# Who splits the shared weight tiles into bf16 pairs, and when the first expert rows are loaded

## The reference

```python
x = x + xattn(layernorm(x), ctx)      # per batch: q, k = ctx @ Wq.T + bq, ctx @ Wk.T + bk
                                      # attention = softmax(q @ k.T); x_m = layernorm(x) @ attention.T
h = layernorm(x)
probs = softmax(h @ gate_w.T)         # 8 experts, the best 2 are kept and renormalised
moe = sum_e combine[e] * (silu(h @ w_gate[e]) * (h @ w_up[e])) @ w_down[e]        # 352 units each
shared = (silu(h @ sw_gate) * (h @ sw_up)) @ sw_down                              # 1408 units
x = x + moe + shared * sigmoid(h @ shared_gate_w)
```

## Time and profile before

| | |
|---|---|
| median of 3 runs | 754.27 us (753.54 to 779.26) |
| the profiled execution | 755.93 us |
| its span in the profile | 754.1 us |
| mean granted clock of TensorE | 0.968 of full speed |
| PE busy | 706.1 us (94%) |
| DVE busy | 344.2 us (46%) |
| ACT busy | 233.7 us (31%) |
| POOL busy | 187.8 us (25%) |
| DMA | 70.99 MB, mean 94 GB/s |

### The profile page before, as it was taken

How to read it: one execution, slowest core, us unless ns; L and a number is a source line. 1 busy time by engine, 2 the same in 40 slices (tenths; PEclk the granted TensorE clock), 3 DMA queues, 4 the chain that set the end, 5 groups by cost and what they waited for, 6 DMA issues and landing times.

```text
span 754.1 us, 10855 instructions
## 1 busy us (share of the span) xinstructions
PE 706.1 (94%) x3808; PEld 381.1 (51%) x3808; DVE 344.2 (46%) x753; ACT 233.7 (31%) x387; POOL 187.8 (25%) x147
## 2 busy tenths in 40 slices
PE   7949979799999999999999899799999999999991
PEld 5525434244454454454444344366666666666660
DVE  3998566514352536452558754363333333333320
ACT  2515013011531132531344343233333333333320
POOL 2372057801400002200244600012222222222221
PEclk8978999899999999999999999899999999999997
DMA  8422022612300003200146972435455445444532
GB/s 281 139 83 84 1 83 85 249 56 84 115 1 0 1 1 112 87 1 1 40 149 226 319 242 76 135 95 90 85 86 86 87 85 86 85 84 87 87 43 28
DMA packets 45749, 70.99 MB, mean 94 GB/s; under 512 B 3577, under 2 KB 25337, under 8 KB 45698
## 3 DMA queue, kind: packets, MB, share of 16 engines
q1 hardware_dynamic: 33570, 41.42, 18.6%
q0 software_dynamic: 10544, 27.30, 16.6%
q10 hardware_dynamic: 1584, 1.57, 0.7%
HBM read 42.99 MB, written 27.29 MB: 93 GB/s over the span
## 4 chain that ended last, share of the span: by engine, by line
PE 83%; DVE 10%; DMA 2%; issue 2%; ACT 1%; SPq 1%; POOL 0%; ACTq 0%; DVEq 0%; POOLq 0%
PE bank L1449 26%; PE bank L1508 19%; PE bank L1464 13%; PE bank L1532 10%; PE bank L1297 4%; PE bank L1496 2%; PE bank L1245 2%; DVE arena L831 2%; PE bank L1519 2%; PE bank L1254 1%; DVE hx_odd L831 1%; PE bank L1267 1%; DVE arena L1135 1%; DMA silu_sb<-L_ffn_shared_gate_w 1%; PE bank L1311 1%
## 5 line engine op out<-in xcount | busy, mean ns | idle before, releaser
L1449 PE MATMUL bank<-hT,arena 128*128 128x512 f16 x1056 | 244.3, 384 | 8.4 <-DVE prod L1152 8.4
L1449 PEld LDWEIGHTS bank<-hT,arena 128*128 128x128 bf16 x1056 | 103.6, 99 | 133.4 <-DVE prod L1152 10.0
L1508 PE MATMUL bank<-arena,ctx_sb 128*128 x936 | 152.2, 312 | 0.0
L1464 PE MATMUL bank<-arena,hidden 128*128 128x512 bf16 x528 | 123.5, 386 | 0.0
L1508 PEld LDWEIGHTS bank<-arena,ctx_sb 128*128 128x128 f16 x936 | 91.2, 97 | 50.0 <-issue 0.2
L570 POOL DMA_INDIRECT out<-staging,token_blk x39 | 60.6, 1553 | 188.3 <-ACT staging L785 184.4
L1197 DVE TENSOR_TENSOR hidden<-bank,hidden 128x384 bf16<-128x384 f32 x39 | 21.7, 557 | 153.9 <-ACT hidden L777 153.9
L1464 PEld LDWEIGHTS bank<-arena,hidden 128*128 128x128 bf16 x528 | 52.1, 99 | 63.4 <-issue 6.7
L1532 PE MATMUL bank<-arena,hidden 128*128 (+1 forms) x351 | 82.2, 379 | 1.5 <-DVE hidden L1197 1.5
L785 ACT ACTIVATE staging<-bank,w_blk 128x512 f32<-128x512 f32 x39 | 26.8, 687 | 122.7 <-PE bank L1532 122.7
L1152 DVE TENSOR_TENSOR prod<-silu_sb,bank 128x512 f32<-128x512 f32 x44 | 30.1, 685 | 73.7 <-PE bank L1449 73.6
(11 more groups left out here) (181 smaller groups left out, 690.4 us busy)
## 6 DMA issues: line engine op xcount, KB each, us to landing
hx_odd<-xs_dram SPq DMA_DIRECT2D x39, 262.0 KB, 2.8
staging<-L_ffn_w_gate SPq DMA_DIRECT2D x6, 704.0 KB, 4.9
staging<-L_ffn_w_up SPq DMA_DIRECT2D x6, 704.0 KB, 5.1
arena<-x SPq DMA_DIRECT2D x3, 1024.0 KB, 7.4
out<-arena POOLq DMA_DIRECT2D x3, 1024.0 KB, 4.7
staging<-L_ffn_w_down SPq DMA_DIRECT2D x6, 512.0 KB, 4.0
staging<-L_ffn_sw_gate SPq DMA_DIRECT2D x11, 256.0 KB, 3.0
staging<-L_ffn_sw_up SPq DMA_DIRECT2D x11, 256.0 KB, 3.5
```

The source lines that it names most:

```text
L1449: op = nc.tensor.matmul(ps[:, :], weights[:, j, wp, kind, c * P:(c + 1) * P], hT[:, t % 2, hp, c, :], start=(c == 0 and s == 0), stop=(c = ...
L1464: op = nc.tensor.matmul(out_ps[i][:, :], hidden[:, j % 3, hp, i * P:(i + 1) * P], weights[:, j, wp, DOWN, :], start=(j == 0 and s == 0), s ...
L1508: op = nc.tensor.matmul(ps[:, 0:I], xT[:, k % 2, xp, c * P:(c + 1) * P], arena[:, bass.ds(at + (part_at(0, part) + wp * low_gap(part) + c ...
```

## The change

It has three parts.

1. POOL splits only tiles 0 to 3 (`POOL_TILES`). Its first split waits for `attn_ready` (batch 0's attention rows scaled), its third for `normed_ready[0]` of batch 1, its fourth for `normed_ready[1]` of batch 0. `routing_constants` stands first.
2. Tiles 4 to 10 are split in block 0 by ACT (`unit_tile_high`) and DVE (`unit_tile_low`) at the points of `TILES_AT`. Each side counts on semaphores of its own, and `wait_split` picks the right one for PE and SP. `assign` moves from (1, "gate") to (1, "down").
3. SP loads the rows of blocks 0 to 2 after 19 pieces of weights instead of after 24.

```diff
@@ AT_POINT_FIRST
-    (1, "gate"): [("assign", 0), ("attn_low", 0)],
+    (1, "gate"): [("attn_low", 0)],
     (1, "up"): [("attn", 0), ("attn", 1), ("attn", 2), ("attn", 3)],
+    (1, "down"): [("assign", 0)],
...
+POOL_TILES = 4
+TILES_AT = {
+    (2, "up"): [4], (3, "up"): [5], (4, "gate"): [6], (5, "up"): [7], (6, "up"): [8], (7, "up"): [9],
+    (8, "up"): [10],
+}
+LOAD_BLOCKS_BEFORE = 19
...
+        def wait_split(eng, j):
+            if j < POOL_TILES:
+                eng.wait_ge(split_pool, j + 1)
+            else:
+                eng.wait_ge(split_dve, j + 1 - POOL_TILES)
...
                 if j >= 2:
-                    sp.wait_ge(split, j - 1)
+                    wait_split(sp, j - 2)
...
+            for q in range(LOAD_BLOCKS_BEFORE):
                 load_piece(q)
-
             sp.wait_ge(table_ready, 1)
...
+            for k in range(3):
+                load_block(k)
+            for q in range(LOAD_BLOCKS_BEFORE, PIECES):
+                load_piece(q)
+            for k in range(3, NBLK):
+                load_block(k)
...
+            routing_constants()
             inverse_deviation(0, 0)
+            pool.wait_ge(attn_ready, RT)
             split_unit_tile(0)
+            split_unit_tile(1)
             inverse_deviation(0, 1)
-            split_unit_tile(1)
-            routing_constants()
+            pool.wait_ge(normed_ready[0], RT * 2)
+            split_unit_tile(2)
             inverse_deviation(1, 0)
-            for j in range(2, 5):
+            pool.wait_ge(normed_ready[1], RT)
+            for j in range(3, POOL_TILES):
                 split_unit_tile(j)
             inverse_deviation(1, 1)
-            for j in range(5, UT):
-                split_unit_tile(j)
             fill_spare()
...
+            def unit_tile_high(j):
+
+                act.wait_ge(staged[j % 2], 16 * 3 * (j // 2 + 1))
+                if j == BORROWED:
+                    act.wait_ge(hlo_ready, KC * 2)
+                nc.scalar.copy(weights[:, j, HI, :, :], staging[:, j % 2, :, :]).then_inc(high_split_act, 1)
...
+                    if t == 0:
+                        for n in TILES_AT.get((j, point), ()):
+                            unit_tile_high(n)
...
+            def unit_tile_low(j):
+
+                dve.wait_ge(high_split_act, j + 1 - POOL_TILES)
+                nc.vector.tensor_tensor(weights[:, j, LO, :, :], staging[:, j % 2, :, :], weights[:, j, HI, :, :],
+                                        ALU.subtract).then_inc(split_dve, 1)
```

More of the change, by code:

```diff
@@ L371, in build_xattn_moe @@
         r_step, exp_in_ready, r_exp = sem("r_step"), sem("exp_in_ready"), sem("r_exp")
-        high_split, split = sem("high_split"), sem("split")
+        high_split_pool, split_pool = sem("high_split_pool"), sem("split_pool")
+        high_split_act, split_dve = sem("high_split_act"), sem("split_dve")
         gate_done, up_done, down_done = sem("gate_done"), sem("up_done"), sem("down_done")
@@ L428, in load_piece @@
                 elif slot < 2:
-                    sp.wait_ge(split, UT)
+                    wait_split(sp, UT - 1)
                 else:
@@ L461, in _, with load_block @@
                 load_unit_tile(j)
-            for q in range(PIECES):
+            def load_block(k):
+                if k >= 3:
+                    sp.wait_ge(xt_turned, k - 2)
+                    sp.wait_ge(meta_ready, k - 2)
+                at = sp.value_load(table[0:1, 0, k:k + 1], min_val=0, max_val=DUMP - P)
+                sp.dma_start(xblk[:, k % 3, :], xs_dram[bass.ds(at, P), :]).then_inc(x_in[k % 3], 16)
+            for q in range(LOAD_BLOCKS_BEFORE):
                 load_piece(q)
@@ L469, in _ @@
             sp.wait_ge(pads_sent, 16 * E)
-            for k in range(NBLK):
-                if k >= 3:
-                    sp.wait_ge(xt_turned, k - 2)
-                    sp.wait_ge(meta_ready, k - 2)
-                at = sp.value_load(table[0:1, 0, k:k + 1], min_val=0, max_val=DUMP - P)
-                sp.dma_start(xblk[:, k % 3, :], xs_dram[bass.ds(at, P), :]).then_inc(x_in[k % 3], 16)
+            for k in range(3):
[4 more added lines that the diff above has]
+                load_block(k)
         @block.gpsimd
@@ L512, in fill_spare @@
                                    pad_row[:, :]).then_inc(spare_filled, 16)
-            arrived = [0, 0]
             def split_unit_tile(j):
                 slot = j % 2
-                arrived[slot] += 16 * 3
-                pool.wait_ge(staged[slot], arrived[slot])
-                if j == BORROWED:
-                    pool.wait_ge(hlo_ready, KC * 2)
-                nc.gpsimd.tensor_copy(weights[:, j, HI, :, :], staging[:, slot, :, :]).then_inc(high_split, 1)
-                pool.wait_ge(high_split, j + 1)
+                pool.wait_ge(staged[slot], 16 * 3 * (j // 2 + 1))
+                nc.gpsimd.tensor_copy(weights[:, j, HI, :, :], staging[:, slot, :, :]).then_inc(high_split_pool, 1)
+                pool.wait_ge(high_split_pool, j + 1)
                 nc.gpsimd.tensor_tensor(weights[:, j, LO, :, :], staging[:, slot, :, :], weights[:, j, HI, :, :],
-                                        ALU.subtract).then_inc(split, 1)
+                                        ALU.subtract).then_inc(split_pool, 1)
             def inverse_deviation(which, b):
@@ L1141, in beside @@
                     attention(t, j, point)
+                    if t == 0:
+                        for n in TILES_AT.get((j, point), ()):
+                            unit_tile_low(n)
                     for q in PIECES_AT.get((t, j, point), ()):
@@ L1474, in ffn_block @@
                 for j in range(UT):
-                    pe.wait_ge(split, j + 1)
+                    wait_split(pe, j)
                     pe.wait_ge(silu_ready, t * UT + PRIME + j)
```

## The result

The changed kernel takes 723.07 us, median of 4 runs (722.17 to 726.31), against 754.9 (753.54 to 779.26) for the kernel before: 0.9593 of its time, 95% interval 0.9559 to 0.9627. The ratio leaves out the run of 779.26, an execution in a slower state of the chip; the median of the other three runs of before is 754.27, and 31.2 us lie between the two kernels. The forecast was 723, range 717 to 732.

What follows compares the result with a forecast made beforehand. PE, busy 94%, was held by waits for DVE, whose SBUF-to-SBUF work waited for POOL's splits. Gains of 9.4 + 6.6 + 8.1 - 0.4 + 7.4 = 31.1 us off the median 754.27 gave 723, range 717 to 732.

Steps and rivals of the forecast that it cites:

- Rival (d): L831 is slow for another reason than POOL, so only the expert entry gains: 747 us; chance 0.03.
- Part 1: Front, to about 60 us: no split beside either slow L831 group, gain 9.4 us, bounds 8 and 11.5.
- Rival (b): Front doesn't gain: POOL's splits slide onto the normalisations or the clock stays low longer, 732 us; chance 0.08.
- Parts 2 and 3: Batch 1's normalisation, gain 6.6 us, and second router, gain 8.1 us: PE's waits there go.
- The cover of 2.2: Batch 1's normalisation: L831 ends 2.2 us before PE finishes its down product; lateness within that costs nothing.
- Part 4: Other moved work: splits on ACT and DVE cost 0, `assign` 0.4 us, the pad fill 0.
- the ring: Two staging slots for unit tiles: a slot's next tile is wanted 15.5 us later, takes 8.2, cover 7 us.
- (a): Tile 6 lands late behind pads and rows, and PE waits 11 us once: 734 us; chance 0.06.
- (c): Turns of the two staging slots take far longer than 8.2 us; at 36 the time is 774 us; chance 0.01.
- Part 5: Expert entry: rows issued ahead of weight piece 19 remove PE's 4.6 us wait; gain 7.4 us, low bound 5.
- what would show it: Signs of being right: L831 near 0.5 us each, no `prod` wait above 1.5, clock 1.00 from 60 on.

Runs made afterwards that it cites:

- e4: Changed kernel plus six GpSimd copies, SBUF to SBUF, beside batch 1's second normalisation: 727.21 us, one run.
- e9: Changed kernel plus six GpSimd memsets, which only write, beside batch 1's second normalisation: 729.73 us, one run.
- e11: Changed kernel with front and expert entry of the kernel before (POOL splits tiles 0 to 4 without waits, rows late): 742.77 us, 0.9833 of before.
- e5: Changed kernel run again unaltered, as yardstick on another chip: 723.55 us, 0.9586 of before.
- e3: Changed kernel without POOL's three waits that hold its splits back: 730.47 us, 0.9686 of before.
- e1: Kernel before with only the rows of blocks 0 to 2 issued after 19 weight pieces: 749.03 us, 0.9931 of before.
- e10: Changed kernel with `assign` back at (1, "gate"): 723.88 us, one run.
- e2: Changed kernel with the rows of blocks 0 to 2 again behind all 24 weight pieces: 730.28 us, 0.9676 of before.
- e6: Changed kernel with POOL splitting only tiles 0 to 2, tile 3 going to ACT and DVE: 722.78 us, 0.9576 of before.
- e8: e7 plus PE turning the shared gate's rows behind batch 0's two projections: 717.53 us, 0.9506 of before.
- e7: e6 plus the routing's `tables` part 2 moved from (2, "gate") to (2, "down") in later blocks: 719.98 us, 0.9535 of before.

## Why the prediction was right

**The bound.** That three of four long waits came from POOL's splits, not from the work of DVE itself, is shown: L831 is back at 1.9 wherever POOL is quiet, and at 6.4 where e4 or e9 makes it busy. That the third of these waits, at the second router, goes with the moved splits is shown by e11. Rival (d) is out.

**Part 1** was 1.1 too small, with the terms off both ways. The 11.2 came whole. L822 lost 1.3 instead of 1.7, because it came 0.96 later than before while the two pairs ended at 35.75, 0.65 later than I had put them; the second L822 lost 0.2 instead of 0.4, L854 0.2 instead of 0.3. That is 9.5; what is left of the 10.53, some 1.0, I put down to the clock, for which I had 0.6. It stayed at full level in this execution (1.00 from 44 to 52), and the first product took 2.75, where the timeline of before has 3.39 (3.19 in the earlier trace rows, by the count of the chain). In e5 it was 0.75 from 46 to 48 and 0.50 from 48 to 50, the product took 3.16 and the stretch 28.89: there the clock's term is 0.5. Rival (b) didn't come, but its mechanism is real: e3, with POOL's waits taken away, has the splits back on the normalisations, and is 7.4 slower, of which 5.9 lie in this stretch.

**Parts 2 and 3** hold within 0.1 as a sum: 14.37 for 14.3 (6.6 + 8.1, less the 0.4 of `assign`), in the changed kernel and again in e11. With the 0.2 that `assign` cost they gave 14.6 for 14.7. The cover of 2.2 was 2.0 (L860 ends at 88.6, PE turns the rows at 90.60). The second router's chain from logits to `prod` is 8.7 us (106.29 to 115.02) for a forecast of some 10, so its cover was 3.3 instead of 3.

**Part 4.** `assign` cost 0.2 for 0.4. The pad fill cost DVE nothing, as taken, though it ran beside L860 itself. No DVE subtraction and no ACT cast made PE wait: the ring never ran dry, and rivals (a) and (c) have nothing in the trace.

**Part 5** gave 7.78 for 7.4, in the changed kernel and in e1 alone. The 0.4 that I had put down as given back by the last splits isn't seen.

**What was wrong.** By the profiled execution the sum was 1.5 too large, 31.1 for 29.6. That the median came within 0.1 us of the forecast is in part luck: the four runs of the changed kernel spread over 4.1 us, and the front's 1.1 too little makes up for what was too much elsewhere. The low end of the range, 717, isn't the sum of the bounds either: their 34.2 gives 720. The step that failed is in "what would show it": the clock at 1.00 from 60 to the end, and no wait for `prod` above 1.5. Block 3's wait of 2.38 stood in the trace of before, hidden in the total of 8.4; I read that group as one place of 4.9 and some crumbs. It was harmless there, since the twelve matmuls behind it took 2.76. In this execution they took 4.35, 1.59 more. The other miss is the start: 0.97 for an edit that doesn't touch it, PE turns the shared gate's rows at 10.68 instead of 9.73, when their load has landed, and the matmuls behind it take as long as before. These two, with +0.45 at the end, -1.1 at the front and -0.4 at the entry, make the 1.5. Both belong to the execution, as far as e5 shows, and not to the change: e5, the same kernel, had its first `mix` at 30.09 and block 3 at full clock, and the profiled run came out at 724.0.

## What to carry to other kernels

When a VectorE instruction's time varies by a factor of five between places, read GpSimd's timeline at the same microseconds before anything else, and sort VectorE's instructions by operand form: PSUM input, two SBUF inputs, one SBUF input. Moving a helper's work away is one way out; making the helper wait until the exposed instruction is through is another, and here three such waits on GpSimd were worth some 7 us (e3), after seven of its eleven tiles had already been moved. Judge a wait of TensorE together with the 2 to 4 us behind it, and open a group of waits into its places even when its largest is explained.

## What the runs showed of the hardware that I had not expected

**The granted clock after one and the same wait isn't the same from run to run.** Block 3's wait of 2.38 us occurs in eleven of the profiled kernels. In five of them (before, e1, e3, e5, e10) the twelve matmuls behind it took 2.76 or 2.77, in six (after, e2, e4, e6, e9, e11) 4.34 to 4.45. Windows of two us there: start and end, PE busy, granted clock, DMA. First the changed kernel as first profiled, then e5, which is the same kernel:

```profile
396.00:398.00 2.00, 1.64 (x4) 0.55 1.06 403
398.00:400.00 2.00, 2.00 (x7) 0.60 1.03 362
400.00:402.00 2.00, 2.00 (x11) 1.00 1.08 389
```

```profile
396.00:398.00 2.00, 2.00 (x10) 1.00 1.04 369
398.00:400.00 2.00, 2.00 (x11) 1.00 1.04 389
```

The same holds at the start, behind the wait for the gate's rows, 2.4 to 3.1 us in all but e10 (4.3). Eight matmuls take 3.70 in e3, e4 and e11, 5.24 in e2, 5.40 in e10, and 6.4 to 6.8 in the others that have this wait, e5 and the first profile among them. In the six kernels that are alike up to there (after, e2, e4, e5, e9, e10) the first `mix` comes anywhere from 26.70 to 31.04, and e2 and e4 waited the same 2.4. Both together are as large as the spread of the changed kernel's runs (722.17 to 726.31). The clock's mean in the profiled execution follows it: 0.985 in the slowest run, 0.988 in the fastest. Where e8 removes the first wait and e7 the second, the range of the four runs shrinks to 0.6 us. What decides which of the two levels follows such a wait, I can't say from these runs.

**POOL is held too.** At 84.22 its rstd on 4 elements per partition takes 2.44 instead of 1.01. Beside it DVE's L1170, which reads two SBUF operands, runs from 84.06 to 85.81, and L547 ends 0.85 behind it. It did no harm, since L860 had 2.0 us of cover.

**A tiny instruction can cost as much as a large one.** L851, 128x4, took 1.49 beside a split, and L883, a scaling of 128x512, 1.52. What it cost was the rest of POOL's instruction (until 35.75 and 49.41), not its own work. That is why e6's move of one split only carried the hold from one small instruction to another.
